# Value products of a graph attention layer: scaled fp16 parts in place of three bf16 parts

## What is computed

```python
q = x @ wq.T + bq;  k = x @ wk.T + bk;  v = x @ wv.T + bv
q2 = (q @ wiq.T + biq).reshape(N, H, D).transpose(1, 0, 2)
k2 = (k @ wik.T + bik).reshape(N, H, D).transpose(1, 0, 2)
v2 = (v @ wiv.T + biv).reshape(N, H, D).transpose(1, 0, 2)
scores = jnp.einsum('hnd,hmd->hnm', q2, k2) / 8 + mask[None]
attn = jax.nn.softmax(scores, axis=-1)
out = jnp.einsum('hnm,hmd->hnd', attn, v2).transpose(1, 0, 2).reshape(N, OUT_F)
x = layernorm(x + out @ wo.T + bo)
```

## Time and profile before

| | us |
|---|---|
| median of 3 runs | 282.12 |
| lowest and highest of them | 281.9, 282.89 |
| the profiled execution, its own time | 282.69 |
| its span, first to last instruction | 280.9 |
| TensorE busy | 274.3 (98%) |
| VectorE busy | 174.6 (62%) |
| ScalarE busy | 153.5 (55%) |
| GpSimd busy | 137.1 (49%) |

### The profile page before, as it was taken

One profiled execution on the slowest core, in us unless ns is written; L12 is line 12 of the kernel. 1 busy time (PEld: TensorE's weight loads), 2 busy tenths in 40 slices (PEclk: granted clock), 3 DMA queues, 4 the chain that ended last, 5 costly groups with the idle time before them and its releaser, 6 DMA issues.

```text
span 280.9 us, 5139 instructions
## 1 busy us (share of the span) xinstructions
PE 274.3 (98%) x1674; PEld 252.6 (90%) x1674; DVE 174.6 (62%) x425; ACT 153.5 (55%) x288; POOL 137.1 (49%) x123
## 2 busy tenths in 40 slices
PE   8999999999999999999999999999999999999992
PEld 8999999999999998888899989889898988787891
DVE  4879976765765676233506687857676577810472
ACT  5973343244244235233318989877879787933221
POOL 2000644565635555533697286483837466497000
PEclk9999999999999999999999999999999999999999
DMA  7949866274474335966404589795867849590032
GB/s 263 341 155 345 290 213 202 98 219 154 122 252 149 91 139 175 350 242 197 153 17 149 108 212 148 228 216 130 228 126 204 163 154 180 166 215 3 9 139 79
DMA packets 51921, 49.31 MB, mean 176 GB/s; under 512 B 41056, under 2 KB 41920, under 8 KB 51776
## 3 DMA queue, kind: packets, MB, share of 16 engines
q1 hardware_dynamic: 49792, 47.63, 58.4%
q0 software_dynamic: 1680, 0.62, 1.1%
q10 hardware_dynamic: 432, 0.85, 0.8%
HBM read 37.44 MB, written 2.21 MB: 141 GB/s over the span
## 4 chain that ended last, share of the span: by engine, by line
PE 98%; DVE 1%; ACT 0%; issue 0%
PE bank L928 24%; PE bank L919 19%; PE bank L921 19%; PE bank L920 19%; PE bank L1025 7%; PE bank L1007 5%; PE bank L944 3%; PE bank L937 1%; ACT res L606 0%; DVE stats L893 0%; DVE res L892 0%; DVE mean_var L895 0%; ACT std L601 0%; DVE scratch L623 0%; DVE rstd L898 0%
## 5 line engine op out<-in xcount | busy, mean ns | idle before, releaser
L387 POOL DMA_INDIRECT mask_cells<-scratch x48 | 53.8, 1120 | 72.1 <-DMA mask_cells<-scratch 29.6
L441 ACT ACTIVATE w_hi<-w_raw 128x1024 fp32r<-128x1024 f32 x49 | 51.5, 1053 | 22.2 <-PE bank L928 19.6
L349 POOL TENSOR_TENSOR w_lo<-w_raw,w_hi 128x1024 fp32r<-128x1024 f32 x17 | 40.8, 2404 | 39.9 <-DVE plane_lo_odd L826 30.4
L919 PE MATMUL bank<-x_hi,w_hi 128*128 128x384 f32 x176 | 58.8, 334 | 0.0
L920 PE MATMUL bank<-x_lo,w_hi 128*128 128x384 f32 x176 | 58.8, 334 | 0.0
L921 PE MATMUL bank<-x_hi,w_lo 128*128 128x384 f32 x176 | 58.8, 334 | 0.0
L633 DVE TENSOR_TENSOR w_lo<-w_raw,w_hi 128x1024 fp32r<-128x1024 f32 x31 | 37.9, 1225 | 16.6 <-ACT w_hi L441 15.6
L484 ACT ACTIVATE h_hi<-bank,bcol 128x384 f32 (+1 forms) x24 | 14.0, 582 | 55.4 <-PE bank L921 52.7
L919 PE MATMUL bank<-h_hi,w_hi 128*128 128x384 f32 x128 | 43.8, 342 | 0.0
L921 PE MATMUL bank<-h_hi,w_lo 128*128 128x384 f32 x128 | 42.8, 335 | 0.0
L920 PE MATMUL bank<-h_lo,w_hi 128*128 128x384 f32 x128 | 42.8, 334 | 0.0
(11 more groups left out here) (99 smaller groups left out, 443.1 us busy)
## 6 DMA issues: line engine op xcount, KB each, us to landing
w_raw<-weights SPq DMA_DIRECT2D x53, 512.0 KB
shared<-key_rows SPq DMA_DIRECT2D x6, 512.0 KB
shared<-start SPq DMA_DIRECT2D x5, 320.0 KB, 6.3
res<-x_rows SPq DMA_DIRECT2D x1, 1536.0 KB
out<-res SPq DMA_DIRECT2D x6, 256.0 KB, 2.2
mask_cells<-scratch POOLq DMA_INDIRECT x48
shared<-start ACTq DMA_DIRECT2D x2, 320.0 KB, 5.2
mask_cells<-mask SPq DMA_DIRECT2D x1, 576.0 KB, 6.0
```

The lines of the kernel that those rows point to most:

```text
L349: nc.gpsimd.tensor_tensor(lo, w_raw[:, s, cols], hi.bitcast(F32), ALU.subtract)\
L387: nc.gpsimd.indirect_dma_start(out=mask_cells, out_offset=bass.IndirectOffsetOnAxis(ap=cell[:, c:c + 1], axis=0), in_=cell_value[:, c:c + ...
L441: nc.scalar.activation(w_part(t, s, slice(0, F))[0], w_raw[:, s, :], ACT.Copy).then_inc(w_hi_done, 1)
L919: pe.matmul(out_ps, w_hi[:, s, cols], moving_hi, start=(k == 0), stop=False)
```

## The change

The scale of a value column is found on the chip. ScalarE writes the absolute values of `v2` as bf16 (`size`, three instructions of 128x1024). TensorE multiplies them by a matrix of ones (`sum_sizes`, six matmuls of 512 columns in banks 4 and 5), which leaves in every partition the sum over all nodes for each of the 1024 features. VectorE takes from it the factor for the attention output, one number per partition and pair (`value_sums`, eight instructions with the identity matrix), scales the sums, and inverts them (`value_scales`, one RECIPROCAL of 128x1024). GpSimd multiplies the values in place (`scale_values`, three instructions of 128x128 a pair), ScalarE writes the fp16 high part, GpSimd one subtraction for the fp16 low part. Three products are left: high planes by both parts, low planes by the high part. `att_high` and `att_low` multiply by `back` in place of a constant.

```diff
-        vp = sb("vp", [P, 2, NT, 2, 3 * D], BF16)
-        v_rest = sb("v_rest", [P, NT, P], F32)
+        vp = sb("vp", [P, 2, 2, NT, P], FP16)
+        v_scale = sb("v_scale", [P, F], F32)
+        back = sb("back", [P, KT], F32)
+        ones = sb("ones", [P, P], BF16)
...
+            def scale_values(a):
+                for n in range(NT):
+                    mine = v2[:, n, ds(a * P, P)]
+                    ins = nc.gpsimd.tensor_tensor(mine, mine, v_scale[:, ds(a * P, P)], ALU.mult)
+                ins.then_inc(v_scaled, 1)
...
-                for n in range(NT):
-                    ins = nc.gpsimd.tensor_tensor(v_rest[:, n, :].rearrange("p (h d) -> p h d", h=2),
-                                                  v_pair(a)[:, n, :, :], v_part(par, 0)[:, n, :, :], ALU.subtract)
-                ins.then_inc(v_step, 1)
...
-                nc.gpsimd.tensor_copy(middle, rest).then_inc(v_step, 1)
-                pool.wait_ge(v_step, 3 * a + 3)
-                nc.gpsimd.tensor_tensor(low, rest, middle, ALU.subtract).then_inc(vp_done, 1)
+                nc.gpsimd.tensor_tensor(v_part(par, 1), v_pair(a), v_part(par, 0), ALU.subtract).then_inc(vp_done, 1)
...
+                elif isinstance(j, int) and j == 1:
+                    pool.wait_ge(scales_made, 1)
+                    scale_values(0)
+                    scale_values(1)
+                else:
+                    v_low(j - 1, 1 - par)
...
+            def size(n):
+                act.wait_ge(v2_ready, 2 * n + 2)
+                nc.scalar.activation(v_size[n], v2[:, n, :], ACT.Abs).then_inc(sizes_made, 1)
...
+            def value_sums():
+                dve.wait_ge(sums_done, 1)
+                for k in range(KT):
+                    col = k * P % HALF
+                    ins = nc.vector.scalar_tensor_tensor(
+                        out=v_scale[:, k * P:(k + 1) * P], in0=size_bank[k * P // HALF][:, col:col + P],
+                        scalar=LEAST, in1=ident[:, :], op0=ALU.max, op1=ALU.mult, accum_out=back[:, k:k + 1])
+                then_settle(ins)
+                nc.vector.tensor_scalar(back[:, :], back[:, :], 1.0 / (FULL * UP), None, ALU.mult)\
+                    .then_inc(back_made, 1)
+                for h, half in enumerate(HALVES):
+                    ins = nc.vector.tensor_scalar(v_scale[:, half], size_bank[h][:, :], LEAST, 1.0 / FULL, ALU.max,
+                                                  ALU.mult)
+                ins.then_inc(sums_read, 1)
+            def value_scales():
+                dve.wait_ge(sums_read, 1)
+                nc.vector.reciprocal(v_scale[:, :], v_scale[:, :]).then_inc(scales_made, 1)
...
                 if isinstance(j, int) and j < 1:
                     evacuate_pair(*q_tile)
+                    value_sums()
                     evacuate_pair(*k_tile)
+                    value_scales()
...
-                for z in range(3):
+                for z in range(2):
                     products(turned_hi, z, start=(z == 0))
...
-                for z in range(2):
-                    products(turned_lo, z, stop=(z == 1))
+                products(turned_lo, 0, stop=True)
+            def sum_sizes():
+                pe.wait_ge(sizes_made, NT)
+                for n in range(NT):
+                    for b, half in zip(size_bank, HALVES):
+                        ins = pe.matmul(b[:, :], ones[:, :], v_size[n][:, half], start=(n == 0), stop=(n == NT - 1))
+                ins.then_inc(sums_done, 1)
```

More of the change, by code:

```diff
@@ L211, in gnn_layer @@
         v2_acc, v2_ready = sem("v2_acc"), sem("v2_ready")
-        vp_hi_done, vp_done = sem("vp_hi_done"), sem("vp_done")
+        sizes_made, sums_done, sums_read = sem("sizes_made"), sem("sums_done"), sem("sums_read")
+        scales_made, back_made = sem("scales_made"), sem("back_made")
+        v_scaled, vp_hi_done, vp_hi_seen, vp_done = (
+            sem(n) for n in ("v_scaled", "vp_hi_done", "vp_hi_seen", "vp_done"))
         scores_seen = sem("scores_seen")
@@ L358, in low_halves @@
                         .then_inc((left_lo_pool, w_lo_pool)[h], 1)
+            def scale_values(a):
[3 more added lines that the diff above has]
+                ins.then_inc(v_scaled, 1)
             def v_low(a, par):
[L362 to L364 removed]
                 pool.wait_ge(vp_hi_done, a + 1)
[L366 to L376 removed]
+                nc.gpsimd.sem_inc(vp_hi_seen, 1)
+                nc.gpsimd.tensor_tensor(v_part(par, 1), v_pair(a), v_part(par, 0), ALU.subtract).then_inc(vp_done, 1)
             pool.wait_ge(table_filled, 16)
@@ L396, in step @@
                 s0 = (2 * par + LEAD) % RING
+                last = isinstance(j, int) and j == PAIRS - 1
                 low_part(t + LEAD, s0)
@@ L410, in step @@
                     low_part(t + LEAD + 1, s0 + 1)
+                if not last and not (isinstance(j, int) and j < 1):
+                    scale_values(j + 1)
             step(0, 0)
             step(1, 1)
+            v_low(0, 0)
             with pool.Fori(1, PAIRS // 2 - 1) as jj:
@@ L551, in step @@
                 more = not (isinstance(j, int) and j < 2)
+                if not attend:
+                    size(0)
+                if isinstance(j, int) and j == 2:
+                    act.wait_ge(back_made, 1)
+                    v_high(0, 0)
                 split(t + LEAD, s0, raws)
-                if attend:
-                    if isinstance(j, int) and a == 0:
-                        act.wait_ge(v2_ready, 2 * NT)
+                if not attend:
+                    for n in range(1, NT):
+                        size(n)
+                if more:
                     v_high(a, 1 - par)
@@ L625, in _ @@
             nc.vector.memset(downs[:, :], 1.0 / UP)
+            nc.vector.memset(ones[:, :], 1.0)
             def low_part(t, s):
@@ L786, in att_low @@
                 nc.vector.scalar_tensor_tensor(
-                    out=att_lo[:, att, :].rearrange("p a n -> p (a n)"), in0=att_bank[:, 0:N], scalar=1.0 / UP,
+                    out=att_lo[:, att, :].rearrange("p a n -> p (a n)"), in0=att_bank[:, 0:N], scalar=back[:, att],
                     in1=att_hi[:, att, :].rearrange("p a n -> p (a n)").bitcast(F32),
@@ L1025, in products @@
                             ins = pe.matmul(att_bank[rows, 0:N].rearrange("p (b q) -> p b q", b=NT),
-                                            vp[:, par, m, h, z * D:(z + 1) * D], turned[:, h, :, m, :],
+                                            vp[:, par, z, m, rows], turned[:, h, :, m, :],
                                             start=(start and m == 0), stop=(stop and m == NT - 1))
@@ L1054, in step @@
                         if start:
+                            if which == 1 and k == 0:
+                                sum_sizes()
                             continue
```

21 lines of the change are left out of this document (13 added, 8 removed).

## The result

The changed kernel takes 287.16 us (median of 4 runs, 286.85 to 287.54) against 282.35 us before on the same chip: ratio 1.0168, 95% interval 1.0151 to 1.0184. It is 4.8 us slower. The prediction was 282.6 us, no change, with a range up to 285.2 us; it was wrong. The profiled execution took 286.85 us, 4.16 us more than that of before.

What follows compares the result with a forecast made beforehand. The prediction took TensorE, busy 98% of the span, as the bound: +1.36 us of new matmuls, about +7.3 us of waits, -8.2 us of products, +0.5 us in all; 282.6 us against the 282.12 us median, range 279.2 to 285.2 us.

Steps and rivals of the forecast that it cites:

- TensorE's own sum: Matmuls removed and added: 8.2 us of value products go, 1.36 us come; a 6.8 us gain were TensorE alone the bound.
- The reciprocal: VectorE's 128x1024 inversion after the low part of k in step 0, priced at 6.8 us; masked scores start about 156.4 us.
- its rival at an ordinary rate: Reciprocal takes only 1.2 us, so the kernel ends 4.5 us earlier, at 277.6 us; chance 0.13.
- that at eight passes: Reciprocal needs 8.3 ns per element, 8.7 us in all; +2.4 us, kernel at 284.5 us; chance 0.13.
- The waits as far as scores(2): TensorE waits behind the late VectorE: 2.2 us at q tile 36, 1.3 us at scores(1), 1.8 us at scores(2).
- D: How much later than before something happens; predicted 6.2 us at attention(0), falling to +0.5 us at the end.
- the slack rule: After scores(2), each step's D is the larger of last D - 1.02 and attention's D - slack (0.66 to 0.98 us).
- one tiny one: Small VectorE instruction in step 0's `value_sums`, priced with eight of 0.29 us and two of 128x512 at some 4 us.
- the rest from the slack rule: TensorE's waits in the steps after scores(2), the remainder of about +7.3 us of waits in all.
- GpSimd's work for a pair falls from 2.6 us to 2.2 us and changes nothing: GpSimd's work per pair, 2.6 us to 2.2 us, claimed to have no effect because GpSimd waits for VectorE anyway.
- The catching up: Rival: with VectorE late, each attention runs 0.4 us shorter, giving 2 us back over five to six steps: 280.5 us; chance 0.15.
- The clock: Rival: TensorE's clock falls from 2.4 to 1.2 GHz after its new waits; +2 us, 284.6 us; chance 0.09.

Runs made afterwards that it cites:

- the reciprocal alone: Kernel before with only a 128x1024 reciprocal (in place on the bias row) added behind the low part of k in step 0: 285.98 us, ratio 1.0141.
- the kernel with no small instruction held up: Changed kernel with its 128x3 row-sum multiplication and 128x8 scaling of `back` in the accumulating form of tensor_scalar: 283.09 us, ratio 1.0031 against the kernel before.
- the one with eight pieces: The kernel with no small instruction held up, its reciprocal cut into eight 128x128 pieces spread over step 0 and attention(0) to attention(2): 280.36 us, ratio 0.991.

## Why the prediction was wrong

**What held.** TensorE's own sum: 18 value matmuls take 1.58 to 1.65 us and the six of `sum_sizes` lengthen the way from tile 32 to scores(0) by 1.32 us (137.97 to 149.81 us against 138.61 to 149.13 us) for 1.36 us. The reciprocal: 6.54 us for 6.8 us; its rival at an ordinary rate (1.2 us) and that at eight passes (8.7 us) are both out. The eight passes came from the Trainium skill, "VectorE: DVE Perf Modes", section "First, the fixed hardware budget", as the prediction says; measured are 6.2 ns per element, 6.0 ordinary passes. That nothing is caught up afterwards: shown by the reciprocal alone, +4.0 us against +3.9 us worked out. The waits as far as scores(2): idle 2.68 us at tile 36 (predicted 2.2 us), 1.04 us in two parts at scores(1) (1.3 us) and 1.64 us at scores(2) (1.8 us); from start to start scores(2) are at D = 6.4 us for a predicted 5.7 us. That the low part of q binds a step: 11.9 us once it is moved. And the slack rule itself, within 0.5 us at every step, once no small instruction is held up.

**The step that failed** is "Less 0.05 us for the semaphore, each step leaves TensorE with D = the larger of (last D - 1.02) and (D of the attention - slack)". It took the slacks of the kernel before as fixed, and so the length of an attention. But the multiplication inside it lasts until GpSimd's running instruction ends, and the change gives GpSimd another instruction there: 0.67 us in steps 4 to 6 in place of 0.16 to 0.47 us, and 1.42 us in step 3 in place of 0.22 us. Steps became 12.58 us where the rule has 12.1 us. The second term with the same fault is "one tiny one" in step 0, priced within some 4 us for all of `value_sums`: it took 2.21 us alone, which put the low part of k behind the sums and the masks 0.85 us later than in the kernel with no small instruction held up. Together this measured 3.9 us (that kernel against the changed one). In the terms of the sum, the waits behind scores(2), "the rest from the slack rule", were put at 2.0 us and are the larger part of the missing 3.7 us (11.0 for 7.3 us): D was above the predicted one by 0.7 us at scores(2), 1.9 us at step 4 and 3.3 us at step 7. Without the hold-ups the time is 0.9 us above before for a predicted +0.5 us.

The sentence "GpSimd's work for a pair falls from 2.6 us to 2.2 us and changes nothing" is the same error from the other side. Less work, but the multiplication now meets a subtraction of 0.93 us where it met a 0.5 us copy or one of three 0.4 us subtractions, and in step 3 a 2.4 us one, and is held up longer each time. The rows to see it were in the trace of before: an instruction of three elements whose mean is 252 ns where its shortest is 149 ns.

**The rivals.** The catching up did not occur; an attention became longer, not shorter. The clock did not fall: after the 2.68 us without a matmul TensorE went on at 0.173 us per 384 columns, the upper level, and the granted clock over the span was 0.996. The rival on the slow side had the wrong mechanism; the right one was not among them.

**Open.** The profiled execution of the changed kernel spends 2.45 us outside its span, that of before 1.79 us, and the other kernels with scaling 2.2 to 2.6 us, but the one with eight pieces 1.76 us. Every kernel without scaling spends 1.7 to 1.8 us there, also the one with the reciprocal added. Spare semaphores do not make it. At the same time the early matmuls reach the upper level of the clock sooner in the changed kernel (two matmuls 0.34 us apart from 5.73 us on, where before they were still 0.64 us apart until 7.06 us), so that its projections are 0.6 us ahead within the span and level with before in the whole time. What links the two is not shown.

## What to carry to other kernels

Before pricing work on VectorE by its size, look at its smallest instructions: if their times scatter by multiples, see what GpSimd runs at that moment, and choose a form that does not wait. Here the accumulating form of tensor_scalar did not, and 17 such instructions were worth 3.9 us; the plain form with one SBUF input did wait (the 128x8 one, 2.21 us). A matmul removed is worth its time only up to the next chain's slack, and that slack is a property of the old timing: 8.2 us of products gave 3.9 us, and 6.0 us once the hold-ups were gone and the low part of q was moved as well. A long instruction on an engine that is idle a third of the time still costs most of its length (4.0 to 4.7 us of 6.54 us) if it stands between two things that the busy engine waits for; in eight pieces, put mostly where the engine waited anyway, it cost 3.4 us less.

## What had not been expected of the hardware

A RECIPROCAL of 128x1024 float32 takes 6.54 us and one of 128x128 0.90 us: for each element of a row some six times the 1.04 ns of an ordinary instruction. Two rows of 128x1 and 128x3 predicted the rate within 5%. An instruction of 128x8 can take 2.21 us, and one of 128x3 1.42 us, when GpSimd is in a 128x1024 instruction. The accumulating form of the same arithmetic takes 0.16 us there. A low plane of 128x384 with two SBUF inputs is held up as well, 1.22 us in place of 0.62 us. An exclusive-or and a bitwise and on 128x512 words of PSUM, one instruction, take 0.64 us, as much as the maximum and the multiplication that they replace.
